# A spectral unit's frequency bins moved half a step: 93 groups for 102, contraction rows filled to 128, tables loaded beside x, matrix sums on two engines

## The chip, the cores and the metric

The kernel runs on one core of a Trainium2 chip. The metric is the device time in microseconds from launch to end. The kernel is one long program of eight stages in a row; the change touches the second of them only. TensorE (PE in the rows) multiplies, VectorE (DVE), ScalarE (ACT) and GpSimd (POOL) copy and compute, SyncE (SP) issues most of the transfers. The column PEclk gives the clock that TensorE was granted, 1.00 for 2.4 GHz and 0.50 for 1.2 GHz.

## The reference, cut to what matters

The second stage takes x as two-dimensional tokens (4 batches, 2304 tokens each, 128 channels), normalises every token, and runs a spectral unit over the token axis for four nested edges of the sequence. In essence:

```
Vf = rfft(phi, n);  Uf = rfft(u, n)           # phi: 2304 x 16 filters, u: b x 2304 x 128
U_plus  = irfft(Vf * Uf)                       # for every filter k and channel d
U_minus = the same for u * (+1, -1, +1, ...)
out  = einsum('btkd,k,kde->bte', U_plus,  sigma**0.25, M_phi_plus)
out += einsum('btkd,k,kde->bte', U_minus, sigma**0.25, M_phi_minus)
out += sum over i < 3 of shift(u, i) @ M_u[i]
```

There are four sets of matrices (M_phi, M_u); a running, weighted sum of them (weights from a softmax with gumbel noise) is what each of the four parts of the spectrum uses. The result is added to x.

## The kernel before, in words

`spectral_unit` (L1056) never forms a filtered signal per k. It evaluates both u and the taps at a set of frequencies ("bins"), builds for each bin a 128 x 128 matrix from taps and M, multiplies, and goes back. Time is written as 64 rows by 36 residues (ROWS_T, RES). Bins are grouped in slots of 36; SEG_SLOTS = (49, 25, 13, 9) slots serve four lengths, and each count is rounded up to a multiple of 3 (TRIO), so there are 17 + 9 + 5 + 3 = 34 trios, 102 slots.

The stage is a sequence of blocks with a barrier after each:

1. `branch_weights` (L1088): eight tiny loads, softmax weights.
2. `load_all`: the four parts of x, nothing else runs.
3. `norm_and_turn` (L138): layer norm on DVE, ACT and POOL. SP loads the tables meanwhile (phi, fa, sign, fe, the first matrices, far).
4. `to_bins` (L1130), the first half: PE turns the taps (L1202), ACT and DVE spread them (L1260, L1262, L1289), PE makes the taps' bins (L1210, contraction over 100 rows: real part in rows 0 to 35, imaginary part in rows 64 to 99), ACT scales and rounds each trio in two instructions (L1267, L1271), DVE takes the rest (L1293), SP stores it (L1340).
5. `to_bins`, the second half, in four phases (2 pairs of batches x 2 halves of the slots, 51 slots each). A phase first turns u (L1222, 16 groups of channels, 64 rows contracted, 51 columns) into tile ax, copied out by ACT (L1276) and DVE (L1298); then, once the last copy is done, bins it (L1234, 17 trios, 100 rows contracted, 72 columns), copied out by ACT (L1280) and DVE (L1302) and stored by SP (L1347).
   Beside it POOL makes the running matrix sum and its rounded high and low parts (L1310 to L1320). After each phase's stores SP stores the matrices to DRAM, the high part twice (six transfers, L1330 and L1331), and loads the next raw ones (L1333, L1334).
6. `mix_bins` (L1362): per trio and half of the output channels, PE fills tile mix (L1432: the matrix load has 105 rows, 216 columns) and multiplies by the bins (L1449), interleaved; ACT and DVE copy out. Both engines' copies are awaited in order by counters. At the first trio and at the three changes of segment ACT loads the matrices, half by half, one transfer of 105 rows by 32 KB for each half (L1503). PE waits for the half that it needs. Each trio's products go to DRAM and come back transposed, and are inverted two trios later (L1459).
7. `from_bins` (L1607): loads the result (L1637, one transfer of 96 rows and one of 6 for each piece), PE contracts it (L1667), DVE adds x (L1675), SP stores.

PE in these blocks follows an order written out by hand; each queue is in order.

Of the kernel before, what the change touches and what calls it, by code (L numbers as in the profile page):

```python
# [137 lines left out]
def norm_and_turn(nc, name, X, XN, eps, ident=None, out_of=None, stores=(), loads=()):  # L138
# [4 lines left out]
    with ExitStack() as ctx:  # L143
# [5 lines left out]
        ps = ctx.enter_context(nc.psum_tensor(name + "_ps", [P, 8, 512], F32))  # L149
        s = Signals(nc, name, "own var_ready std_ready shift_ready by_dve by_act by_pool turned held stored fetched")  # L150
# [14 lines left out]
        with nc.Block() as block:  # L165
            @block.sync
            def _(sp):
                for dst, src in loads:
                    sp.dma_start(dst, src).then_inc(s["fetched"], 16)
# [8 lines left out]
                if loads:  # L178
                    sp.wait_ge(s["fetched"], 16 * len(loads))
# [876 lines left out]
def spectral_unit(nc, x_dram, out_dram, w, scratch):  # L1056

    bins_dram, taps_dram = scratch("fq_bins", [TRIOS, P, 2, WORDS]), scratch("fq_taps", [TRIOS, TALL_M, COLS])
    mats_dram = scratch("fq_mats", [NEDGE, TALL_M, C * P])
    prod_dram, back_dram = scratch("fq_prod", [SLOTS_F * RES, 8, C]), scratch("fq_back", [RES, 2 * SLOTS_F, B * C])  # L1060
    with ExitStack() as ctx:
        def sb(name, shape, dt=F32):
            return ctx.enter_context(nc.sbuf_tensor("fq_" + name, shape, dt))

        wgt, root = sb("wgt", [P, NEDGE]), sb("root", [STACK, 1])
        branch_weights(nc, w, wgt, root)
        with ExitStack() as held:
            def part(name, shape, dt=F32):
                return held.enter_context(nc.sbuf_tensor("fq_" + name, shape, dt))

            U, turned = part("u", [P, G, 2, C]), part("ax", [P, HALF_SLOTS * 2 * C])
            fe, fa, sign = part("fe", [TALL, SLOTS_F, 2 * RES]), part("fa", [P, 2, SLOTS_F]), part("sign", [TALL, 1])
            far, far_r = part("far", [LAGS * TRIOS, LAGS * COLS]), part("far_r", [LAGS * TRIOS, LAGS * COLS], F32R)
            mats = [part("mats_" + n, [P, C * P // 4], dt) for n, dt in (("raw", F32), ("sum", F32), ("high", F32R), ("low", F32R))]
            lags = [part("lags_" + n, [32 * LAGS, C * P // 32], dt) for n, dt in (("raw", F32), ("sum", F32), ("high", F32R), ("low", F32R))]
            phi = turned[0:ROWS_T, SLOTS_F * STACK:SLOTS_F * STACK + RES * NK]
            flat = U[:, :, :, :].rearrange("p g t c -> p (g t) c")
            load_all(nc, "fq_load", [(flat[ROWS_T * (b % 2):ROWS_T * (b % 2) + ROWS_T, RES * (b // 2):RES * (b // 2) + RES, :],
                                      x_dram[b * S:(b + 1) * S, :].rearrange("(a r) c -> a r c", r=RES)) for b in range(B)])
            norm_and_turn(nc, "fq_ln", U[:, :, :, :], U[:, :, :, :], 1e-5, loads=[  # L1080
                (phi, w["phi"]), (fa[:, :, :], w["fa"]), (sign[:, :], w["sign"]), (fe[:, :, :], w["fe"]),
                (mats[0][:, :], w["mats"][0]), (lags[0][:, :], w["lags"][0]), (far[:, :], w["far"])])
            to_bins(nc, w, U, turned, fe, fa, sign, phi, far, far_r, mats, lags, wgt, root, bins_dram, taps_dram, mats_dram)
        mix_bins(nc, w, bins_dram, taps_dram, mats_dram, prod_dram, back_dram)
# [2264 lines left out]
```

## Time and profile before

| | us |
|---|---|
| median of 3 runs | 9376.89 (9366.43 to 9382.52) |
| the profiled execution | 9381.17 |
| its span, first to last instruction | 9378.6 |
| mean granted TensorE clock | 0.887 |

The profiled execution lies 4.3 us above the median of the runs; 2.6 us of it lie outside the span. The spectral unit takes from about 4225.9 to 6037.2 us of the span. A row of a table by stretches gives, after the length of the stretch, each engine's busy time with the number of its instructions in brackets, the granted clock, the mean busy share of the 16 DMA engines, and their GB/s.

### The profile page before, as it was taken

Reading aid. Unit: us, or ns where it says so; the run is one execution under the profiler, and the core shown is the slowest. Engines: PE = TensorE matmul, PEld = TensorE weight load, DVE = VectorE, ACT = ScalarE, POOL = GpSimd, SP = SyncE. Lnnn points to the kernel's source line nnn. Section 1 sums busy time; section 2 is a strip of 40 time slices with the busy share of each in tenths; the row PEclk is TensorE's granted clock in tenths of the full one; section 3 lists DMA queues with packets and bytes.
Section 4 is the critical chain, followed back from the end, with each engine's and each line's share of the span. In section 5 each row is a group of like instructions: output and inputs, shape, how many; then the busy total and the mean of one; then the engine's idle time right before and its main releaser. Section 6 shows DMA issues by size and latency. Waiting matters only on the chain. (4 is left out here: it accounts for less than half of the span.)

```text
span 9378.6 us, 167204 instructions
## 1 busy us (share of the span) xinstructions
PE 7377.9 (79%) x63268; PEld 4812.3 (51%) x63268; DVE 6500.1 (69%) x8252; ACT 4637.2 (49%) x8709; POOL 4163.0 (44%) x2920
## 2 busy tenths in 40 slices
PE   5877778777778777875799999388499989995667
PEld 3444444444444344444788888166355555553455
DVE  7999899998999799993166555232376656633447
ACT  4666566665666466652156555124224444452431
POOL 4999599995999499983300000000100000010001
PEclk8999999999999999995699999699679999997778
DMA  4555355553555355544332333621300010003000
GB/s 145 165 165 165 92 177 164 163 151 119 165 165 165 91 175 165 165 128 151 134 74 60 89 86 86 160 71 45 143 21 16 21 36 16 16 1 148 21 23 20
DMA packets 470862, 976.30 MB, mean 104 GB/s; under 512 B 127918, under 2 KB 226549, under 8 KB 452983
## 3 DMA queue, kind: packets, MB, share of 16 engines
q1 hardware_dynamic: 469098, 938.10, 33.6%
q10 hardware_dynamic: 960, 27.53, 1.1%
q8 instruction: 501, 8.21, 0.4%
q14 instruction: 303, 2.47, 0.1%
HBM read 822.05 MB, written 114.81 MB: 100 GB/s over the span
## 5 line engine op out<-in xcount | busy, mean ns | idle before, releaser
L892 POOL TENSOR_TENSOR ss_work<-ss_dtu,ss_ringb 128x768 f32<-128x768 f32 x1536 | 2759.6, 1822 | 260.0 <-POOLq L59 256.6
L754 PE MATMUL ss_ps<-ss_work,ss_ident 128*128 128x512 f32 (+1 forms) x6144 | 2307.9, 521 | 615.5 <-POOL ss_work L902 600.0
L754 PEld LDWEIGHTS ss_ps<-ss_work,ss_ident 128*128 128x128 f32 x6144 | 1201.0, 203 | 1503.5 <-issue 1319.0
L876 DVE TENSOR_TENSOR_SCAN ss_work<-ss_ps,ss_last,ss_work 128x768 f32<-128x768 f32 x1024 | 1808.6, 1800 | 64.2 <-ACT ss_ps L807 53.2
L807 ACT ACTIVATE ss_ps<-ss_dt,ss_a_neg 128x768 f32<-128x768 f32 x1536 | 1374.6, 895 | 288.1 <-DVE ss_work L876 270.9
L861 DVE TENSOR_TENSOR ss_work<-ss_work,ss_ps 128x1152 f32<-128x1152 f32 x768 | 1019.0, 1327 | 1.2 <-ACT ss_ps L815 1.2
L2655 DVE TENSOR_REDUCE at_top<-at_ps 128x1 f32<-128x384 f32 x1512 | 728.1, 546 | 402.5 <-PE at_ps L2573 402.3
L2636 ACT ACTIVATE at_probs<-at_ps 128x768 f32<-128x768 f32 x864 | 653.6, 808 | 660.4 <-PE at_ps L2592 659.4
L876 DVE TENSOR_TENSOR_SCAN ss_work<-ss_ps,ss_work 128x768 f32<-128x768 f32 x512 | 878.1, 1742 | 51.4 <-issue 18.0
L1409 DVE COPY mb_mix<-mb_ps 128x432 f32<-128x432 f32 x1088 | 634.4, 632 | 400.5 <-PE mb_ps L1432 400.4
L1499 ACT ACTIVATE mb_mix<-mb_ps 128x432 f32<-128x432 f32 x1088 | 612.6, 619 | 435.0 <-PE mb_ps L1432 429.0
L902 POOL TENSOR_TENSOR ss_work<-ss_work,ss_ringc 128x384 f32<-128x384 f32 x768 | 772.4, 1006 | 22.1 <-DVE ss_work L876 22.1
L1432 PE MATMUL mb_ps<-mb_taps,mb_mats 105*128 105x216 f32 x4352 | 668.1, 298 | 28.8 <-DMA mb_mats<-fq_mats 24.8
L2602 PE MATMUL at_ps<-at_probs,at_v 128*64 128x384 f32 x3456 | 663.5, 506 | 0.0
L1432 PEld LDWEIGHTS mb_ps<-mb_taps,mb_mats 105*128 105x128 f32 x4352 | 549.0, 196 | 128.3 <-issue 78.1
L2558 POOL COPY at_inv<-at_kept 32x384 f32<-32x384 f32 x80 | 39.9, 499 | 1224.3 <-ACT at_kept L2641 1222.7
L1449 PE MATMUL mb_ps<-mb_mix,mb_bins 128*8 128x64 f32 x29376 | 522.3, 221 | 30.7 <-issue 30.5
L1492 POOL COPY mb_bins<-mb_bins_by 128x432 f32<-128x432 f32 x34 | 20.3, 596 | 1182.6 <-PE mb_ps L1449 1049.6
L2573 PE MATMUL at_ps<-at_packs 96*128 96x384 f32 x1512 | 496.9, 379 | 19.6 <-DMA at_packs<-at_high 19.1
L813 ACT ACTIVATE ss_ps<-ss_ringc 128x512 f32<-128x512 f32 x768 | 462.7, 603 | 83.3 <-DVE ss_work L861 80.1
L2592 PE MATMUL at_ps<-at_packs 128*128 128x384 f32 x1728 | 453.0, 355 | 53.2 <-PEq L59 40.2
L1449 PEld LDWEIGHTS mb_ps<-mb_mix,mb_bins 128*8 128x8 f32 x29376 | 420.2, 90 | 94.8 <-issue 36.1
(554 smaller groups left out, 9917.5 us busy)
## 6 DMA issues: line engine op xcount, KB each, us to landing
ss_ringb<-scan_rows SPq DMA_DIRECT2D x768, 384.0 KB, 3.6
ss_ringc<-scan_rows SPq DMA_DIRECT2D x768, 384.0 KB, 3.9
c_w<-in_l_ffn_w SPq DMA_DIRECT2D x52, 1024.0 KB, 12.3
mb_mats<-fq_mats ACTq DMA_DIRECT2D x8, 3360.0 KB, 17.3
at_packs<-at_high SPq DMA_DIRECT2D x64, 288.0 KB, 5.5
fq_mats<-fq_mats_high SPq DMA_DIRECT2D x8, 2048.0 KB, 9.8
fq_bins<-tb_out SPq DMA_DIRECT2D x68, 216.0 KB, 1.9
mb_bins_by<-fq_bins SPq DMA_DIRECT2D x34, 432.0 KB, 3.9
```

The costliest lines, as they stand in the source:

```text
L754: return pe.matmul(acc[:, d * WIN + a:d * WIN + e], ident[:, :], weighed[:, t % DEEP, d, a:e], start=n == 0 and e - a == 512, stop=n == NS ...
L807: act.activation(decay[d], dt[:, i % 2, d, :], ACT.Exp, scale=a_neg[:, SECTIONS[i][0], d, n:n + 1]).then_inc(s["decayed"], 1)
L861: dve.tensor_tensor(weighed[:, t % DEEP, :, 0:SPLIT], hid[:, t % DEEP, :, 0:SPLIT], bc(spread_c[:, None, :], [P, D2, SPLIT]), ALU.mult).th ...
L876: dve.tensor_tensor_scan(hid[:, t % DEEP, d, ::step], decay[d][:, ::step], drive[:, t % DEEP, d, ::step], start, ALU.mult, ALU.add).then_i ...
L892: pool.tensor_tensor(drive[:, t % DEEP, d, :], dtu[:, t // NST % 2, d, :], ringb[:, t % RING, :], ALU.mult).then_inc(s["driven"], 1)
L902: pool.tensor_tensor(weighed[:, t % DEEP, :, SPLIT:WIN], hid[:, t % DEEP, :, SPLIT:WIN], bc(ringc[:, t % RING, None, SPLIT:WIN], [P, D2, W ...
L1409: copy(*fill_part(h, n)).then_inc(sem, 1)
L1432: ins = pe.matmul(ps[:, n % 4, e * COLS:(e + 1) * COLS], mats[:, first:first + P], taps[:, c % 2, :], start=True, stop=True, skip_group_ch ...
L1449: ins = pe.matmul(ps[32 * g:32 * g + 8, 4 + y % 2, at:at + HALF_E], bins[:, c % 2, n, 1 - m:3 - m, :].rearrange("p m b -> p (m b)"), mix[: ...
L2602: ins = pe.matmul(acc[64 * h:64 * h + 64, 0:R], v[:, j, 2 * pair + h, :, :].rearrange("p a d -> p (a d)"), probs[:, n % 4, h, :], start=j ...
L2636: act.activation(probs[:, n % 4, :, :], ps[:, 2 * (n % 2):2 * (n % 2) + 2, 0:R], ACT.Exp).then_inc(s["weighed"], 1)
L2655: dve.tensor_reduce(top[:, bass.ds(tile + h * NT_, 1), u], ps_bank(ps, 5 + g % 3)[:, 0:R], AX.X, ALU.max).then_inc(s["reduced"], 1)
```

## The change

- Bins at odd half steps. `frequency_tables` puts the frequencies at (2 f + 1) / 2 instead of f, so that no slot holds a bin that is its own mirror. SEG_SLOTS = (48, 24, 12, 9): 16 + 8 + 4 + 3 = 31 trios, 93 slots, with no slot left empty. The two halves of the slots are now 16 trios (48 slots) and 15 (45 slots).
- Contraction rows filled. Tables fe and sign get 128 rows (rows 36 to 63 and 100 to 127 of fe are zero); the turned tiles are copied out with 128 rows, and DVE blanks PSUM rows 32 to 63 and 96 to 127 first. L1234's and L1210's matmuls contract over 128 rows.
- Another order of blocks. `branch_weights`, the load of x and the taps' half of `to_bins` become one block, `taps_to_bins`, ahead of the layer norm. Everything that SP loads is issued at its start on SP's queue. Each tap trio is rounded by one ACT instruction and one DVE instruction that reads PSUM. The first matrices' sum is made at its end by DVE and ACT.
- Matrix sums on DVE and ACT, in five pieces, in the midst of the binning of phases 0 to 2; POOL does nothing there. The high part is stored once (four transfers), the raw load goes ahead of the stores.
- `mix_bins` reads the high part twice: six transfers where there was one. At the start the first half comes in four pieces, the first issued by ACT, the others, the bins and the second half by SP.
- `from_bins` splits the slots at 48: one transfer of 96 or 90 rows for each piece.

```diff
-SEG_SLOTS = (49, 25, 13, 9)
+SEG_SLOTS = (48, 24, 12, 9)
-SEG_TRIOS = tuple(-(-n // TRIO) for n in SEG_SLOTS)
+SEG_TRIOS = tuple(n // TRIO for n in SEG_SLOTS)
+PART_TRIOS = ((TRIOS + 1) // 2, TRIOS // 2)
+ROWS_K = P
-            fe, fa, sign = part("fe", [TALL, SLOTS_F, 2 * RES]), part("fa", [P, 2, SLOTS_F]), part("sign", [TALL, 1])
+        fe, fa, sign = part("fe", [ROWS_K, SLOTS_F, 2 * RES]), part("fa", [P, 2, SLOTS_F]), part("sign", [ROWS_K, 1])
+        taps_to_bins(nc, w, x_dram, ps, U, turned, fe, fa, sign, far, far_r, mats, lags, wgt, root, taps_dram)
+        norm_and_turn(nc, "fq_ln", U[:, :, :, :], U[:, :, :, :], 1e-5)
+        to_bins(nc, w, ps, U, turned, fe, fa, mats, lags, wgt, bins_dram, mats_dram)
...
+            def _(sp):                                   # taps_to_bins
+                for dst, src in ((phi, w["phi"]), (fa[:, :, :], w["fa"])):
+                    sp.dma_start(dst, src).then_inc(s["phi_loaded"], 16)
+                for dst, src in few:
+                    sp.dma_start(dst, src).then_inc(s["few_loaded"], 16)
+                sp.dma_start(sign[:, :], w["sign"]).then_inc(s["few_loaded"], 16)
+                sp.dma_start(fe[:, :, :], w["fe"]).then_inc(s["fe_loaded"], 16)
+                for b in range(B):
...
+                sp.dma_start(far[:, :], w["far"]).then_inc(s["far_loaded"], 16)
+                for dst, src in ((mats[0][:, :], w["mats"][0]), (lags[0][:, :], w["lags"][0])):
+                    sp.dma_start(dst, src).then_inc(s["mats_loaded"], 16)
+                for n in range(TRIOS):
+                    sp.wait_ge(s["lowered"], n + 1)
+                    sp.dma_start(taps_dram[n, 0:STACK, :], split[:, n % RING_T, :].bitcast(F32)).then_inc(s[stored[n % RING_T]], 16)
...
+                for n in range(TRIOS):                    # its ACT part
+                    act.wait_ge(s["made"], GROUPS_K + n + 1)
+                    if n >= RING_T:
+                        act.wait_ge(s[stored[n % RING_T]], 16 * (n // RING_T))
+                    act.activation(split[:, n % RING_T, :], bank(GROUPS_K + n)[0:STACK, 0:COLS], ACT.Copy, scale=root[:, :]).then_inc(s["rounded"], 1)
...
+                for rows in (slice(32, 64), slice(96, 128)):   # its DVE part
+                    dve.memset(ps[rows, :, :], 0.0).then_inc(s["blank"], 1)
...
+                    dve.scalar_tensor_tensor(low, bank(GROUPS_K + n)[TAPS:2 * TAPS, 0:COLS], root[TAPS:2 * TAPS, :], low, ALU.mult, ALU.subtract).then_inc(s["lowered"], 1)
+                dve.wait_ge(s["mats_loaded"], 32)
+                for q in range(PIECES):
+                    raw, total_m = pieces[q][0], pieces[q][1]
+                    dve.tensor_scalar(total_m, raw, wgt[0:raw.shape[0], 0:1], None, ALU.mult).then_inc(s["summed"], 1)
+                for q in range(PIECES):
+                    dve.wait_ge(s["cut"], q + 1)
+                    dve.tensor_tensor(pieces[q][3], pieces[q][1], pieces[q][2], ALU.subtract).then_inc(s["cut_low"], 1)
...
                         act.activation(*binned_part(ph, i), ACT.Copy).then_inc(s["by_act"], 1)
+                        if ph + 1 < NEDGE and i // 2 < PIECES:
+                            cut(ph, i // 2)
...
                         dve.tensor_copy(*binned_part(ph, i)).then_inc(s["by_dve"], 1)
+                        q = i // 2
+                        if ph + 1 < NEDGE and q < PIECES:
+                            if q + 1 < PIECES:
+                                gather(ph, q + 1)
+                            lower(ph, q)
-            @block.gpsimd
...
-                    for i, (source, source_l) in enumerate(((high, high_l), (high, high_l), (low, low_l))):
+                    for i in range(2):
+                        sp.dma_start(mats_dram[n, i, 0:TAPS, :].rearrange("j (q x) -> (j q) x", q=4), mats[2 + i][:, :].bitcast(F32)).then_inc(s["mats_stored"], 16)
+                        sp.dma_start(mats_dram[n, i, TAPS:TAPS + LAGS, :].rearrange("l (g x) -> (l g) x", g=32), lags[2 + i][:, :].bitcast(F32)).then_inc(s["mats_stored"], 16)
...
+        def load_mats(eng, n, first, end, sem):          # mix_bins
+            part = slice(first * PIECE, end * PIECE)
+            taps_high, taps_low = (mats_dram[n, i, 0:TAPS, part] for i in range(2))
+            lags_high, lags_low = (mats_dram[n, i, TAPS:TAPS + LAGS, part] for i in range(2))
+            at = 0
+            for source in (taps_high, taps_high, taps_low, lags_high, lags_high, lags_low):
+                rows = source.shape[0]
+                eng.dma_start(mats[at:at + rows, part].bitcast(F32), source).then_inc(sem, 16)
+                at += rows
...
-                load_mats(0, 0)
-                load_mats(0, 1)
+                load_mats(act, 0, 0, 1, s["mats_first"])
...
                 load_taps(0)
+                for q in range(1, FIRST_LOADS):
+                    load_mats(sp, 0, q, q + 1, first_loads[q])
                 load_bins(0)
+                load_mats(sp, 0, FIRST_LOADS, 2 * FIRST_LOADS, s["mats_second_half"])
...
-                            for lo, hi in ((0, 96), (96, SLOTS_F)):
-                                rows = back_dram[first:first + STEP, SLOTS_F * half + lo:SLOTS_F * half + hi, :].rearrange("i p x -> p i x")
-                                sp.dma_start(Z[lo:hi, n % RING_Z, half, u, :, :], rows).then_inc(s[loaded[n % RING_Z]], 16)
+                            rows = back_dram[first:first + STEP, PART_ROWS[0] * half:PART_ROWS[0] * half + PART_ROWS[half], :].rearrange("i p x -> p i x")
+                            sp.dma_start(Z[0:PART_ROWS[half], n % RING_Z, half, u, :, :], rows).then_inc(s[loaded[n % RING_Z]], 16)
```

## Rows read from the trace of the kernel before

**Rows 1.** By stretches: us; PE, PEld, DVE, ACT, POOL busy; PEclk, DMA share, GB/s.
```profile
4225.90:4235.20 9.30, 0.00 (x0) 0.00 (x0) 1.92 (x12) 2.08 (x5) 0.00 (x0) 0.50 0.02 1
4235.20:4261.10 25.90, 0.00 (x0) 0.00 (x0) 0.00 (x0) 0.00 (x0) 0.00 (x0) 0.50 0.86 182
4261.10:4295.40 34.30, 0.00 (x0) 0.00 (x0) 27.95 (x136) 8.24 (x22) 14.77 (x19) 0.50 0.64 168
4295.40:4346.80 51.40, 39.07 (x269) 38.18 (x270) 29.60 (x36) 30.35 (x71) 28.13 (x6) 0.50 0.20 56
4346.80:4388.10 41.30, 24.01 (x1025) 22.59 (x1025) 9.90 (x18) 8.78 (x18) 12.05 (x2) 0.58 0.61 231
4388.10:4431.50 43.40, 43.39 (x204) 43.40 (x204) 4.86 (x8) 4.24 (x8) 24.61 (x7) 0.50 0.22 83
4431.50:4470.80 39.30, 23.93 (x1026) 22.59 (x1025) 9.32 (x16) 8.72 (x17) 10.61 (x1) 0.68 0.63 242
4470.80:4512.20 41.40, 41.32 (x204) 41.28 (x204) 4.86 (x8) 4.24 (x8) 26.00 (x8) 0.53 0.24 86
4512.20:4552.90 40.70, 23.63 (x1025) 22.47 (x1024) 9.32 (x16) 8.71 (x17) 11.42 (x2) 0.81 0.61 234
4552.90:4594.50 41.60, 41.54 (x205) 41.44 (x205) 4.86 (x8) 4.24 (x8) 25.18 (x7) 0.53 0.23 86
4594.50:4632.20 37.70, 23.59 (x1027) 22.61 (x1027) 9.32 (x16) 8.73 (x17) 0.00 (x0) 0.75 0.49 192
4632.20:4674.80 42.60, 41.82 (x204) 41.62 (x203) 4.86 (x8) 4.77 (x9) 0.00 (x0) 0.52 0.23 84
...
4730.00:5907.00 1177.00, 1139.85 (x33419) 965.33 (x33418) 712.42 (x1226) 698.22 (x1258) 77.92 (x96) 0.99 0.30 76
5924.80:6037.20 112.40, 30.30 (x144) 5.94 (x144) 12.37 (x18) 0.00 (x0) 0.00 (x0) 0.56 1.00 218
```

**Rows 2.** SP in order of time, at two successive trios of the mixing.
```profile
5003.17 0.33 SPq L1547 DMA_DIRECT2D mb_taps<-fq_taps  x1
...
5036.87 0.33 SPq L1547 DMA_DIRECT2D mb_taps<-fq_taps  x1
```

**Rows 3.** PE in order of time, within the turning of u: start, length, idle before.
```profile
4358.36 2.97 PE L1222 MATMUL tb_ps<-fq_fa,fq_u 64*36 64x51 f32 x127 [4.70 <-issue]
...
4544.77 2.89 PE L1222 MATMUL tb_ps<-fq_fa,fq_u 64*36 64x51 f32 x127 [0.60 <-issue]
```

**Rows 4.** Transfers from 4346 to 4380 us: KB each, us from issue to landing.
```profile
fq_taps<-fq_ax SPq DMA_DIRECT2D x3, 81.0 KB, 2.5
fq_lags_raw<-in_l_ffn_lags SPq DMA_DIRECT2D x1, 192.0 KB, 18.9
```

**Rows 5.** Three lines alone by stretches, the binning (L1234), L2140 and L2299.
```profile
4552.90:4555.30 2.40, 2.34 (x21) 2.37 (x22) 1.00 0.03 7
...
6547.30:6563.90 16.60, 16.24 (x144) 16.11 (x144) 1.00 0.02 8
...
6649.00:6677.00 28.00, 28.00 (x143) 28.00 (x143) 0.50 0.01 2
```

**Rows 6.** Instructions of L2140 and L2299: count, ns, rows by columns.
```profile
L2140 PE MATMUL c1p_ps<-c1p_wt,c_xn x144: 222/275/323, 6547.3 to 6563.8; 128*128 128x64 f32 x144
...
L2299 PE MATMUL c1s_ps<-c1s_rows,c_weights x144: 417/417/578, 6648.6 to 6677.2; 64*128 64x128 f32 x144
```

**Rows 7.** The matmuls of the taps' bins: ns min, median, max; first and last.
```profile
L1210 PE MATMUL tb_ps<-fq_fe,fq_ax x204: 367/368/435, 4313.0 to 4346.5; 100*96 100x72 f32 x102
```

**Rows 8.** From the page, a long DVE tensor operation: busy, mean ns, idle before.
```profile
L861 DVE TENSOR_TENSOR ss_work<-ss_work,ss_ps 128x1152 f32<-128x1152 f32 x768 | 1019.0, 1327 | 1.2 <-ACT ss_ps L815 1.2
```

**Rows 9.** PE in order of time, at the start of mixing and a change of segment.
```profile
4712.76 2.05 PE L1432 MATMUL mb_ps<-mb_taps,mb_mats 105*128 105x216 f32 x8 [1.79 <-DMA mb_mats<-fq_mats]
...
5268.55 0.63 PE L1432 MATMUL mb_ps<-mb_taps,mb_mats 105*128 105x216 f32 x2 [4.00 <-issue]
```

**Rows 10.** From the page, the matrices' loads: count, KB each, us to landing.
```profile
mb_mats<-fq_mats ACTq DMA_DIRECT2D x8, 3360.0 KB, 17.3
```

More of the change, by code:

```diff
@@ L1058, in spectral_unit @@
     bins_dram, taps_dram = scratch("fq_bins", [TRIOS, P, 2, WORDS]), scratch("fq_taps", [TRIOS, TALL_M, COLS])
-    mats_dram = scratch("fq_mats", [NEDGE, TALL_M, C * P])
+    mats_dram = scratch("fq_mats", [NEDGE, 2, TAPS + LAGS, C * P])
     prod_dram, back_dram = scratch("fq_prod", [SLOTS_F * RES, 8, C]), scratch("fq_back", [RES, 2 * SLOTS_F, B * C])
[L1061 to L1071, printed above, removed]
-            fe, fa, sign = part("fe", [TALL, SLOTS_F, 2 * RES]), part("fa", [P, 2, SLOTS_F]), part("sign", [TALL, 1])
[L1073 to L1084, printed above, removed]
@@ new lines, in spectral_unit, with matrix_pieces, taps_to_bins @@
+    mix_bins(nc, w, bins_dram, taps_dram, mats_dram, prod_dram, back_dram)
+    from_bins(nc, w, back_dram, x_dram, out_dram)
+def matrix_pieces(mats, lags):
+    width = C * P // 16
+    return [[m[:, q * width:(q + 1) * width] for m in mats] for q in range(4)] + [[m[:, :] for m in lags]]
+PIECES = 5
+def taps_to_bins(nc, w, x_dram, ps, U, turned, fe, fa, sign, far, far_r, mats, lags, wgt, root, taps_dram):
+    GROUPS_K, RING_T = NK // 4, 8
+    flat = U[:, :, :, :].rearrange("p g t c -> p (g t) c")
+    taps = turned[:, 0:SLOTS_F * STACK].rearrange("p (n k) -> p n k", k=STACK)
+    phi = turned[0:ROWS_T, SLOTS_F * STACK:SLOTS_F * STACK + RES * NK]
+    by_lag = phi.rearrange("a (r k) -> a r k", k=NK)
+    at = SLOTS_F * STACK + RES * NK
+    split = turned[0:STACK, at:at + RING_T * COLS].rearrange("p (n x) -> p n x", x=COLS).bitcast(F32R)
+    pieces = matrix_pieces(mats, lags)
+    sigma = w["sigma"].rearrange("(k a) -> k a", a=1)
@@ L1099, in branch_weights @@
-        s = Signals(nc, "bw", "own max_ready exp_ready root")
-        with nc.Block() as block:
+        lw, gum, e = sb("lw", [P, NEDGE]), sb("gum", [P, NEDGE]), sb("e", [P, NEDGE])
+        mx, total, hard, count = sb("mx", [P, 1]), sb("total", [P, 1]), sb("hard", [P, NEDGE]), sb("count", [P, NEDGE])
+        ones = sb("ones", [P, NEDGE])
+        stored = [f"stored{n}" for n in range(RING_T)]
+        s = Signals(nc, "tt", " ".join(["own few_loaded phi_loaded fe_loaded x_loaded far_loaded mats_loaded blank max_ready exp_ready root made by_act by_dve copied spread rounded lowered far_rounded far_stored weighted summed cut cut_low", *stored]))
@@ new lines, in _ @@
+                dve.wait_ge(s["copied"], 1)
+                dve.tensor_copy(taps[:, :, TAPS:2 * TAPS], taps[:, :, 0:TAPS]).then_inc(s["spread"], 1)
+                for n in range(TRIOS):
+                    dve.wait_ge(s["rounded"], n + 1)
+                    low = split[TAPS:2 * TAPS, n % RING_T, :]
+                    dve.scalar_tensor_tensor(low, bank(GROUPS_K + n)[TAPS:2 * TAPS, 0:COLS], root[TAPS:2 * TAPS, :], low, ALU.mult, ALU.subtract).then_inc(s["lowered"], 1)
+                dve.wait_ge(s["mats_loaded"], 32)
@@ new lines, in to_bins @@
+def to_bins(nc, w, ps, U, turned, fe, fa, mats, lags, wgt, bins_dram, mats_dram):
+    CG = C // 8
+    RING_B = 4
+    PHASES = 4
+    flat = U[:, :, :, :].rearrange("p g t c -> p (g t) c")
+    ax = turned[:, :].rearrange("p (n r c) -> p n r c", r=2, c=C)
+    pieces = matrix_pieces(mats, lags)
+    starts = [0]
+    for ph in range(PHASES):
+        starts.append(starts[-1] + 2 * CG + PART_TRIOS[ph % 2])
+    def owner(n):
+        ph = max(p for p in range(PHASES) if starts[p] <= n)
+        v = n - starts[ph]
@@ L1184, in ax_free @@
         def ax_free(eng, ph):
-            eng.wait_ge(s["made"], turned_at(ph, 0, 0))
-            if ph == 0:
-                for n in range(RING_T):
-                    eng.wait_ge(s[stored_t[n]], 16 * len(range(n, TRIOS, RING_T)))
+            if ph:
+                eng.wait_ge(s["made"], turned_at(ph, 0, 0))
         with nc.Block() as block:
```

333 lines of the change are left out of this document (161 added, 172 removed).

## The prediction, made before the changed kernel was run

> **What bounds the kernel now.** I read the granted clock and the page first, then cut the spectral unit into stretches by its barriers, then looked at PE in order of time in each, and last at the transfers. All that the change touches lies between 4225.9 and 6037.2 us. The table by stretches [rows 1] shows four different limits, and the reader should see them apart.
> - Up to 4346.8 us there is a serial chain: tiny loads 9.3, x 25.9 with no engine at work, layer norm 34.3, taps 51.4. Sum 120.9 us.
> - Then four phases, each a turning of u (41.3, 39.3, 40.7 and 37.7 us, PE busy in 24 of them) and a binning (43.4, 41.4, 41.6, 42.6 us, PE busy throughout, yet at clock 0.50 to 0.53). The turning is held by PE's instructions not coming: "issue" gaps of 4.7 us while the DMA engines carry the matrices, 0.6 us when they don't [rows 3].
> - The mixing, 1177 us, is PE at clock 0.99, 97% busy, 33.7 us for a trio (5036.87 - 5003.17 [rows 2]).
> - The last block, 112.4 us, has a DMA share of 1.00: bytes bound it.
>
> **Fewer trios in the mixing.** 34 become 31 with nothing else changed within a trio: 3 x 33.7 = -101 us. Nothing hides it, since PE is the bound.
>
> **Its matrix loads.** The bytes stay; one transfer of 105 rows becomes six, issued by ACT between copies that PE waits for. At a change of segment a half takes 17.3 us to land [rows 10], about PE's half trio of 33.7 / 2, and the gap that PE shows there is one for its instructions, 4.00 us [rows 9], not one for the matrices. Five more issues at about 0.33 us (the issue time of rows 2) hold ACT 1.7 us, six times; most is covered by four banks of PSUM. I take +3 us (0 to +25 if landing grows by 4 us in each of the six). At the start, the second half decides: PE got past it at 4712.76 [rows 9], 38 us after the binning's end, for 6.9 MB plus bins. The first half in pieces lets PE begin earlier and then wait for the same landing. So the early start is worth nothing; I take +3 us (-3 to +9) for smaller transfers.
> A rule of the Trainium skill speaks against this part (page "DMA: Bandwidth & Descriptors", section "Why a DMA increments its semaphore by 16 and not by 1"): a copy is spread over the largest number of engines, at most 16, that divides its outer sizes. By it the 3-row parts sit on three engines, which then carry 9 rows in place of 7 for each half; as an estimate from that page and rows 10, landing goes from 17.3 to 22 us. By that the start would lose 8 us and the changes of segment next to nothing. No row of before has such a 3-row load.
>
> **Fewer and other binnings.** A phase had 17 trios of 12 matmul records; 204 in 43.4 us [rows 1] is 213 ns each at clock 0.50, 2.56 us for a trio. With 62 for 68: 6 x 2.56 = -15 us. DVE and ACT get the matrix sums here: pieces of 1024 columns cost 1.2 us on DVE (1.33 us for 1152 [rows 8]); ACT has one such piece where DVE has two. Beside one 0.61 us copy (4.86 us for 8 [rows 1]) for two trios, DVE has 3.0 us of work in 5.1 us. Hidden, at the low clock.
>
> **The clock in the binning.** This is the disputed step. In the high stretch 22 records took 2.40 us, 109 ns each [rows 5], half the price. Phases 1 to 3 began high, but by their means of 0.53, 0.53 and 0.52 over 41 to 43 us [rows 1] they were high for 2 to 3 us only. Which streams of short matmuls keep the clock? L2140 has 128 rows and 64 columns and kept 1.00 for all of its 16.6 us; L2299 has 64 rows and 128 columns, more column time, and stayed at 0.50 for 28 us, fully busy [rows 5, 6]. The binning has 100 rows and 72 columns. So rows seem to count, and with 128 it is closer to the stream that kept its clock. But neither row shows such a stream climbing by itself from 0.50; it has to enter high, over the short wait for the last copies. Turnings were at 0.58, 0.68, 0.81 and 0.75 on average [rows 1], so perhaps half of the phases enter high and hold. A phase that holds saves 15.5 trios x 1.28 = 20 us, less the 2 us that it had: 18 us. I take two: -36 us (0 to -72). In such a phase DVE's 3.0 us stand against PE's 2.6 for two trios, for five pairs: 2 us late, taken up by eight banks.
> The Trainium skill's rule (page "TensorE: Matmul & The Clock Gate", section "Part 1: The HAM clock gate") is that sustained activity releases the throttle, without a word on rows. The trace disagrees: PE is busy for 43.39 of 43.40 us at 0.50. By the rule as written the filled rows would change nothing, and the step would be worth 0 instead of -36.
>
> **The turning.** 48 or 45 columns for 51 change nothing, since PE waits for instructions. The transfers beside it go from 9.2 MB (three stores of 2.1 MB with three thin ones of 0.2, and a raw load of 2.3) to 6.9, in the last phase from 6.9 to 4.6. At the free pace (2.9 + 0.6 us for two groups [rows 3], 8 times) a turning takes 28 us; the four took 159, 47 us more, for 34.4 MB. In proportion to bytes 25.3 MB cost 34: -13 us (-25 to 0). ax has 128 rows for 100 in its copies: columns set the copy time, no cost.
>
> **The head.** Now one block. SP puts 10.9 MB on its queue at once (fe 3.4, x 4.7, matrices 2.3, rest), at 182 to 212 GB/s: 55 us. The taps took 17.6 us from the block's start to their first binning (4295.4 to 4313.0 [rows 1, 7]); a second blanking of 4096 columns adds at most 4.7 us by L861's rate [rows 8], so eight trios are binned by 30 us. Then the ring of eight is full, and its stores stand in SP's queue behind the loads, as fq_lags_raw's 192 KB took 18.9 us behind the matrices where 81 KB took 2.5 on a queue nearly idle [rows 4]. At 57 us the stores land. PE is ahead by eight banks; 15 trios are left at 6 x 164 ns (204 in 33.5 us [rows 7]), 15 us: 72. DVE reaches the matrices only then: five sums and five differences, 10 us: 82; stores of far and the barrier: 86. Then the layer norm, 34.3, as before: 120. Against 120.9: 0 us (-12 to +12). What was to hide behind the load of x is late again for the queue's order. No loads run beside the norm, which gains nothing: DVE and POOL bound it.
>
> **The last block.** It is bound by bytes: 15.0 MB of 24.5 shrink by 9/102, 1.3 MB at 218 GB/s [rows 1] is -6 us, and the 6-row transfers go: -7 us (-12 to -3).
>
> **Sum**, against the profiled execution: -101 + 3 + 3 - 15 - 36 - 13 + 0 - 7 = -166 us. From 9381.2 that is 9215; the median of the runs is 4.3 us lower: 9211 us.
>
> **Rivals.**
> 1. The clock stays low in all binnings, because one drop lasts to the phase's end: -130 us, 9247. For it: each of the three high entries fell within 3 us [rows 1]; the skill's rule above gives the same. Against: L2140.
> 2. The clock holds in all four: -202 us, 9175. For it: less traffic makes the turnings denser, so they enter high more often. Against: the first turning was mostly low.
> 3. The matrix loads land late and PE waits, +4 us in six halves and +9 at the start instead of +6 together, with the head 12 us longer and at most one phase high: 9275. For it: six transfers for one, all to be landed. Against: the gap at a change names PE's instructions, not the matrices [rows 9].
> 4. Slower than before: the clock falls at a change of segment and doesn't come back in the mixing. At half the clock a trio takes at most 67.4 us, 33.7 more. From five such trios on the whole gain is gone; if it were ten of the fifteen after the first change, 337 us: 9548. For it: longer waits for instructions at a change (4.00 us [rows 9]) are what the clock would fall after. Against: the mean clock of the mixing is 0.99 [rows 1], so it came back each time.
> 5. That the change does not do what it says, fewer trios at another period: each trio does the same work, so I give it nothing of its own.
>
> **Chances.** Forecast (one to three phases high) 0.42; none 0.28; all four 0.16; rival 3 0.12; rival 4 0.02. The forecast's own range is 9188 to 9237. The range that should hold the time 8 times in 10 takes in rivals 1 and 2: 9168 to 9265. About 0.2%, 19 us, is what can be told from no change. Faster 0.97, within 0.2% 0.01, slower 0.02.
>
> **What would show it.** In the mixing 31 taps loads at 33.7 us: wrong if the period moves. In the binnings PEclk and the length: about 20 us at 1.00, 40 at 0.50; the first microseconds of each tell whether it entered high. In the turnings fewer gaps over 3 us. In the head: the first tap stores landing after the matrices; if they land early, the block ends 10 to 15 us sooner. At the start of the mixing PE's wait before the second half, at about 34 us after the first issue. The forecast fails if the layer norm starts later than 95 us after the block's start, or if PE waits for mb_mats at the changes.

## The result and the profile after

The changed kernel takes 9313.35 us (median of 14 runs, 9266.97 to 9338.35) where the kernel before takes 9379.95 (14 runs, 9345.20 to 9400.23): ratio 0.9927, 95% interval 0.9913 to 0.9940. That is 67 us faster, not the 169 us of the forecast (9211), and outside its range of 9168 to 9265. The profiled execution took 9326.6 us, its span is 9324.8.

The changed kernel by stretches, answering [rows 1] (columns as there). In order: the head's block, the layer norm, four times turning and binning, the wait for the matrices, the first trio, the rest of the mixing, the last block.

```profile
4228.70:4309.80 81.10, 31.32 (x250) 30.73 (x250) 32.57 (x58) 24.73 (x46) 0.00 (x0) 0.58 0.63 170
4309.80:4342.40 32.60, 0.00 (x0) 0.00 (x0) 27.96 (x136) 8.19 (x21) 14.75 (x18) 0.50 0.00 1
4342.40:4381.30 38.90, 23.68 (x1024) 22.40 (x1024) 8.96 (x17) 7.84 (x16) 0.00 (x0) 0.50 0.49 180
4381.30:4422.50 41.20, 41.14 (x193) 41.04 (x193) 14.78 (x17) 8.53 (x13) 0.00 (x0) 0.50 0.22 82
4422.50:4459.60 37.10, 23.49 (x1025) 22.38 (x1024) 9.20 (x18) 7.53 (x16) 0.00 (x0) 0.71 0.51 195
4459.60:4497.20 37.60, 37.56 (x182) 37.46 (x182) 14.75 (x17) 8.00 (x12) 0.00 (x0) 0.52 0.23 83
4497.20:4535.00 37.80, 23.55 (x1025) 22.31 (x1025) 9.01 (x17) 8.39 (x17) 0.00 (x0) 0.64 0.51 191
4535.00:4576.10 41.10, 41.09 (x192) 41.01 (x192) 14.72 (x17) 8.53 (x13) 0.00 (x0) 0.50 0.22 82
4576.10:4612.30 36.20, 23.68 (x1025) 22.44 (x1024) 9.13 (x17) 7.53 (x16) 0.00 (x0) 0.59 0.35 136
4612.30:4651.00 38.70, 38.65 (x180) 38.47 (x180) 4.25 (x7) 3.71 (x7) 0.00 (x0) 0.50 0.22 81
4651.00:4668.90 17.90, 0.00 (x0) 0.03 (x1) 0.91 (x1) 0.53 (x1) 0.00 (x0) 0.50 0.77 169
4668.90:4722.80 53.90, 32.19 (x561) 29.71 (x561) 19.77 (x33) 18.92 (x34) 4.84 (x6) 0.62 0.48 100
4722.80:5833.10 1110.30, 1036.71 (x29890) 879.34 (x29886) 644.31 (x1108) 628.31 (x1137) 70.58 (x87) 0.96 0.31 74
5867.90:5974.40 106.50, 31.16 (x144) 5.95 (x144) 12.38 (x18) 0.00 (x0) 0.00 (x0) 0.56 1.00 218
```

Three things are to be seen. No binning was at a clock above 0.50 for more than 2 us. The first trio takes 53.9 us, with PE busy in 32 of them. The mixing's clock is 0.96 where it was 0.99, and PE is busy for 1037 of 1110 us (93%, before 97%).

The mixing again, before and after, from the second trio to the last fill: PE's groups with their idle time and what ended it. First the kernel before.

```profile
L1432 PE MATMUL mb_ps<-mb_taps,mb_mats 105*128 105x216 f32 x4220 | 642.7, 296 | 4.0 <-issue 4.0
L1449 PE MATMUL mb_ps<-mb_mix,mb_bins 128*8 128x64 f32 x28488 | 506.4, 221 | 26.2 <-issue 26.0
L1459 PE MATMUL mb_ps<-mb_prod_t,mb_fi 72*100 72x512 f32 x192 | 107.7, 643 | 0.1
```

The changed kernel:

```profile
L1491 PE MATMUL mb_ps<-mb_taps,mb_mats 105*128 105x216 f32 x3839 | 592.7, 298 | 32.4 <-ACT mb_mix L1562 17.3 <-issue 14.4 <-DVE mb_mix L1468 0.7
L1508 PE MATMUL mb_ps<-mb_mix,mb_bins 128*8 128x64 f32 x25920 | 463.7, 222 | 22.0 <-issue 22.0
L1518 PE MATMUL mb_ps<-mb_prod_t,mb_fi 72*100 72x512 f32 x174 | 98.5, 648 | 19.1 <-DMA mb_fi<-in_l_ffn_fi 19.1
```

Idle time goes from 30 to 74 us, and nobody names the matrices. Four single rows of PE and ACT in the changed kernel tell where: at the mixing's start, then at the second and third change of segment.

```profile
4704.90 2.04 PE L1491 MATMUL mb_ps<-mb_taps,mb_mats 105*128 105x216 f32 x8 [20.43 <-DMA mb_mats<-fq_mats]
...
5562.83 0.54 ACT L1562 ACTIVATE mb_prod<-mb_ps 104x448 f32<-104x448 f32 x1 [18.98 <-DMA fq_prod<-mb_prod]
...
5564.34 1.62 PE L1491 MATMUL mb_ps<-mb_taps,mb_mats 105*128 105x216 f32 x6 [12.98 <-ACT mb_mix L1562]
...
5733.19 2.03 PE L1518 MATMUL mb_ps<-mb_prod_t,mb_fi 72*100 72x512 f32 x2 [19.15 <-DMA mb_fi<-in_l_ffn_fi]
```

ACT waits 19 us to reuse a product buffer, because a 14 KB store has not landed; PE waits for ACT; PE waits for an 84 KB load. These small transfers share the DMA engines with the six loads of a half. (With one load for a half it can happen too, more seldom: in the run f3 below PE waited 13.2 us for the same 84 KB load.)

Away from the changes the period is what it was [rows 2]: SP's loads of taps in the changed kernel, two undisturbed ones and then across the first change (45.7 and 48.4 us).

```profile
4992.59 0.33 SPq L1608 DMA_DIRECT2D mb_taps<-fq_taps  x1
5026.26 0.33 SPq L1608 DMA_DIRECT2D mb_taps<-fq_taps  x1
...
5195.92 0.33 SPq L1608 DMA_DIRECT2D mb_taps<-fq_taps  x1
5241.60 0.33 SPq L1608 DMA_DIRECT2D mb_taps<-fq_taps  x1
5290.00 0.33 SPq L1608 DMA_DIRECT2D mb_taps<-fq_taps  x1
```

Below, "excess" is the sum over all trios but the last of (start of the next trio's first fill - start of its own - 33.7 us). It is 48 us before and 120 after, 20 of them in the first trio. It is read from the one profiled execution of each kernel. Kernels that load their matrices alike differ by up to 11 us (changed, e3 and e4: 120, 111, 113; e2, f2, f4 and g4: 55, 47, 58, 47; before and f3: 48, 58).

### The profile page after: what moved, and what is told of

Its sections match the earlier page's. It is cut to its first block and busy times, and to the rows that moved or that the text cites. A ratio compares the mean times of both kernels' runs of the same rounds, so it can differ in the third digit from the quotient of the medians.

```text
span 9324.8 us, 160533 instructions
## 1 busy us (share of the span) xinstructions
PE 7266.0 (78%) x60184; PEld 4717.3 (51%) x60184; DVE 6468.1 (69%) x8177; ACT 4579.4 (49%) x8574; POOL 4017.7 (43%) x2881
## 5 line engine op out<-in xcount | busy, mean ns | idle before, releaser
L872 DVE TENSOR_TENSOR_SCAN ss_work<-ss_ps,ss_work 128x768 f32<-128x768 f32 x512 | 878.9, 1745 | 51.7 <-issue 17.3
L1468 DVE COPY mb_mix<-mb_ps 128x432 f32<-128x432 f32 x992 | 578.8, 631 | 427.0 <-PE mb_ps L1491 426.7
L1562 ACT ACTIVATE mb_mix<-mb_ps 128x432 f32<-128x432 f32 x992 | 557.2, 617 | 442.5 <-PE mb_ps L1491 437.1
L1491 PE MATMUL mb_ps<-mb_taps,mb_mats 105*128 105x216 f32 x3968 | 617.6, 300 | 72.0 <-DMA mb_mats<-fq_mats 39.6
L1491 PEld LDWEIGHTS mb_ps<-mb_taps,mb_mats 105*128 105x128 f32 x3968 | 507.8, 198 | 164.9 <-issue 81.8
L1508 PE MATMUL mb_ps<-mb_mix,mb_bins 128*8 128x64 f32 x26784 | 478.7, 222 | 25.3 <-issue 25.3
L2655 PE MATMUL at_ps<-at_packs 128*128 128x384 f32 x1728 | 452.2, 354 | 53.8 <-PEq L59 40.0
L1508 PEld LDWEIGHTS mb_ps<-mb_mix,mb_bins 128*8 128x8 f32 x26784 | 386.0, 91 | 83.3 <-issue 30.8
```

Of the source, the lines that this page charges most:

```text
L872: dve.tensor_tensor_scan(hid[:, t % DEEP, d, ::step], decay[d][:, ::step], drive[:, t % DEEP, d, ::step], start, ALU.mult, ALU.add).then_i ...
L1468: copy(*fill_part(h, n)).then_inc(sem, 1)
L1491: ins = pe.matmul(ps[:, n % 4, e * COLS:(e + 1) * COLS], mats[:, first:first + P], taps[:, c % 2, :], start=True, stop=True, skip_group_ch ...
L1508: ins = pe.matmul(ps[32 * g:32 * g + 8, 4 + y % 2, at:at + HALF_E], bins[:, c % 2, n, 1 - m:3 - m, :].rearrange("p m b -> p (m b)"), mix[: ...
```

## The experiments

Ratios are to the kernel before, with their 95% intervals; landing is from the first to the last packet of the first half of the matrices at the first change of segment, in the profiled execution.

| kernel | runs | median us | ratio | excess | landing us |
|---|---|---|---|---|---|
| changed | 14 | 9313 | 0.9927 (0.9913-0.9940) | 120 | 24.7 |
| e1, 32+16+16+16+16+9 rows | 12 | 9323 | 0.9954 (0.9937-0.9971) | 160 | 28.0 |
| e2, one of 105 rows | 6 | 9225 | 0.9860 (0.9835-0.9884) | 55 | 14.2 |
| e3, x on ACT's queue | 6 | 9303 | 0.9930 (0.9906-0.9954) | 111 | 24.0 |
| e4, 16 long matmuls | 3 | 9299 | 0.9928 (0.9900-0.9956) | 113 | 23.5 |
| e5, before + six loads | 6 | 9436 | 1.0065 (1.0049-1.0082) | 100 | 24.4 |
| f2, six of 105 rows, by columns | 5 | 9217 | 0.9834 (0.9816-0.9852) | 47 | 14.8 |
| f3, before + 16 long | 8 | 9368 | 0.9993 (0.9978-1.0007) | 58 | 15.2 |
| f4, e2 + 4 long | 5 | 9186 | 0.9805 (0.9785-0.9824) | 58 | 14.2 |
| g1, 32+32+32+9 rows | 4 | 9255 | 0.9879 (0.9861-0.9898) | 100 | 20.4 |
| p1, 0-63, 64-95, 96-104 | 2 | 9271 | 0.9899 (0.9875-0.9922) | 113 | 19.8 |
| p2, 0-31, 32-95, 96-104 | 2 | 9254 | 0.9881 (0.9856-0.9905) | 63 | 15.7 |
| g4, f4 + matmuls at the start | 5 | 9192 | 0.9813 (0.9797-0.9829) | 47 | 14.1 |

The kernel before has an excess of 48 and a landing of 15.6 us.

**e1: no three-row loads.** Edit:

```
-            for source in (taps_high, taps_high, taps_low, lags_high, lags_high, lags_low):
+            for source in (taps_high, taps_high[0:half], taps_high[half:TAPS], taps_low[0:half], taps_low[half:TAPS], mats_dram[1][n, :, part]):
```

> The changed kernel, still with six loads for each half of the matrices, but no part of 3 rows: 32, 16, 16, 16, 16 and one of 9 (the lags' high sums are stored twice for it, 0.2 MB more a segment). Theory A, three-row parts: in the changed kernel a half took 24 us to land (5214.0 to 5238.0) instead of 17.3, with three 3-row copies one after another at the end while the DMA share fell; PE's instructions and the product stores stood behind them, and the clock fell. By A a half lands in 17 us, the sum of the trios' excess over 33.7 us goes from 120 back to about 50, the kernel 50 to 70 us faster than the changed one: ratio to before 0.987. Rival B, the number of transfers (ACT issues for 2.8 us instead of 0.3, six landings to wait for): no change, 0.993. Rival C, chance of the clock at each change: within 10 us of the changed kernel, with other trios long.

Measured: not faster than the changed kernel but, if anything, slower (the two intervals just touch), excess 160. My first theory fell: without a 3-row part a half lands still later, after 28.0 us. The stretches of the trace say why; first the 32-row part of e1, then its 16-row parts.

```profile
5182.40:5187.20 4.80, 4.10 (x117) 3.54 (x114) 2.41 (x4) 2.28 (x5) 0.55 (x1) 1.00 1.06 220
5187.20:5205.00 17.80, 7.03 (x134) 6.14 (x135) 3.20 (x6) 2.20 (x4) 0.00 (x0) 0.62 1.06 130
```

The DMA engines are full in both, but 16-row parts move 130 GB/s where the 32-row part moves 220.

**e2: one load of 105 rows.** Edit, with the stores as in the kernel before:

```
-            for source in (taps_high, taps_high, ...): eng.dma_start(mats[at:at + rows, part]..., source)
+            eng.dma_start(mats[:, part].bitcast(F32), mats_dram[n, :, part]).then_inc(sem, 16)
```

> The changed kernel with the matrices stored as before (high sums twice, six stores, 35 rows more a segment) and loaded by one transfer of 105 rows for a half (one for each quarter of the first half). A and B both expect the excess of the trios back at about 50 us and 50 to 70 us gained, less 3 us for the stores in the turnings: ratio to before 0.987. C expects no change. If it is faster than the run with six loads of 16 or 32 rows, the difference is the number of transfers.

Measured: 0.9860, excess 55. The loads' form so costs some 65 us of excess. That the median fell by 88 us and not by 65 has two more reasons in the trace: PE's first fill came 9.7 us after the last binning (17.9 in the changed kernel), and three binnings held the high clock, of which more under e4. The same stretch of time in the changed kernel (32-row parts, then the 3-row ones) and in e2:

```profile
5214.10:5229.20 15.10, 7.91 (x189) 6.88 (x190) 4.44 (x8) 3.60 (x7) 0.42 (x1) 0.76 0.98 205
...
5229.00:5238.00 9.00, 8.68 (x238) 7.54 (x237) 4.84 (x9) 4.92 (x9) 0.00 (x0) 0.82 0.66 111
```

```profile
5162.60:5176.00 13.40, 11.32 (x264) 8.65 (x264) 6.23 (x11) 5.51 (x10) 0.00 (x0) 0.90 0.99 262
```

205 and then 111 GB/s against 262. With its stores as before (six transfers for four) the turnings took 158.4 us again, where the changed kernel has 150.0. The other traces divide in the same way: kernels with the six stores (f2, f4, g4, p1, p2) have 158 to 160 us, those that store the high part's 32 rows once (e1, e3, e4, g1) 147 to 150.

**e5 and f2: the number of loads against the rows they span.** e5 takes the kernel before and cuts its load in six by rows; f2 takes e2 and cuts it in six by columns:

```
+                    for lo, hi in ((0, TAPS), (TAPS, 2 * TAPS), (2 * TAPS, STACK), (STACK, STACK + LAGS), ...):   # e5
+                        act.dma_start(mats[lo:hi, part].bitcast(F32), mats_dram[n, lo:hi, part])...
+                for q in range(6):                                                                                # f2
+                    part = slice(first * PIECE + 1408 * q, min(first * PIECE + 1408 * (q + 1), end * PIECE))
```

> The kernel before, each half of the matrices loaded by six transfers (32, 32, 32, 3, 3 and 3 rows) in place of one of 105; nothing else. Theory D (the rate of a transfer goes by how many rows of SBUF it spans: with 105 rows 262 GB/s in the changed kernel with one load, with 32 rows 203 to 220, with 16 rows 130): the trios' excess over 33.7 us goes from 48 to 100 or more at the changes and 15 us come at the start, so the kernel before gets 50 to 70 us slower, ratio 1.006. Theory B (the number of transfers): the same here. Rival E (it is the source in DRAM, where the changed kernel reads the same rows twice and from another stride): no change here, since the source stays as it was, ratio 1.000.

> The changed kernel with the matrices stored as before and each later half loaded by six transfers of all 105 rows, each of 1408 of the 8192 columns. By D as fast as with one load of 105 rows: excess about 55 us, ratio 0.986 (0.984 to 0.989). By B (six issues by ACT, six landings) as slow as the changed kernel: excess 100 to 120 us, ratio 0.992 or more.

Measured: e5 is 61 us slower than the kernel before (1.0065): 52 us more excess, and PE's first fill 33.0 us after the last binning where it was 23.0. So this one edit, alone, costs what the changed kernel lost. The source in DRAM was untouched, so it is not the source. f2 issues six loads as well and is as fast as e2 (0.9834), so it is not the number of transfers either. Left are the rows that a load spans in SBUF, the memory that the kernel's tiles lie in.

**p1 and p2: which rows.** `cuts = (0, 64, 96, 105)` against `(0, 32, 96, 105)` in e2.

> Each later half loaded as rows 0 to 63, 64 to 95 and 96 to 104, from the array as stored before. The Trainium skill (page SBUF, section on the DMA port swizzle) says that partitions 0 to 63 reach the same 8 ports as 0 to 31, and 32 to 95 all 16. By it the 64-row load moves at the 32-row load's rate, 205 GB/s, 10 us. Rival (the rate goes by the number of rows alone): 64 rows at some 235 GB/s, 9 us, and the same in the next kernel.

> The same three sizes in another place: rows 0 to 31, 32 to 95 and 96 to 104. By the port map the 64-row load now moves at the rate of the 105-row one, 262 GB/s, in 8 us, 2 us less than where it spans rows 0 to 63; a half lands 2 us earlier and the kernel is 0 to 15 us faster. By the number of rows alone: no difference between the two.

Within the 64-row load, p1 and p2:

```profile
5176.20:5180.80 4.60, 0.82 (x17) 0.53 (x16) 1.00 (x2) 1.09 (x2) 0.00 (x0) 0.81 1.01 207
```

```profile
5209.80:5214.20 4.40, 0.94 (x18) 0.65 (x17) 1.12 (x2) 1.09 (x2) 0.00 (x0) 0.77 1.10 432
```

The same 64 rows' worth of bytes: 207 GB/s into rows 0 to 63, 432 into rows 32 to 95, where the expectation had 262. Excess 113 against 63. So the number of rows alone doesn't set the rate. The times (9271 and 9254, two runs each) can't be told apart: in p1's profiled run two binnings held the high clock, in p2's none, which makes up for most of the difference in excess. The Trainium skill's map (page "SBUF — State Buffer", section "Door 1: The DMA port swizzle (why `[64,N]` ≈ `[32,N]`)") gives rows 0 to 15 four ports of sixteen, 0 to 31 and 0 to 63 eight, 64 to 127 the other eight; the trace agrees with 130 GB/s for 16-row loads, 205 for 32 rows and 207 for rows 0 to 63, and with 432 where rows 32 to 95 take in both eights. The map alone doesn't explain one load of 105 rows, which takes in both eights as well and ran at 262; why is not shown.

**g1: the 3-row tail apart.** One load of 9 rows for three of 3.

> The changed kernel with the three 3-row loads of a half made one of 9 rows (the lags' high sums stored twice for it), so four loads: 32, 32, 32 and 9. It parts the cost of the 32-row spans from that of the 3-row tail. If the spans cost most, three of them take 3 x 5.1 us at 205 GB/s and the 9 rows 3 us, landing about 19 us in place of 24 (and 13.4 with one load): excess of the trios 85 to 95 us, ratio 0.990. If the three 3-row loads were all of the cost: excess 55, ratio 0.986. If they cost nothing: excess 115 to 120, 0.993.

Measured: excess 100, landing 20.4. Of the 65 us between 120 and 55 the 3-row loads make 20 (11 by the 111 of e3, which has the same loads as the changed kernel), the 32-row spans some 45.

The table's last two columns read together: a half has half a trio, 33.7 / 2 = 16.9 us, to land before PE comes to it. The kernels that land in 14.1 to 15.7 us have an excess of 47 to 63, those that take 19.8 to 28.0 have 100 to 160.

**e3: x on another queue.** The loads of x, far and the first matrices issued by ACT (`sp.dma_start` becomes `act.dma_start`).

> The changed kernel with the loads of x, of the far taps and of the first matrices issued by ACT, so that the tap stores on SP's queue stand only behind fe. Theory A (a queue's order): the ring of eight is not held up, PE's gap of 18.8 us in the taps' binning goes, the layer norm begins 15 to 20 us earlier (65 us after the block's start instead of 81), time 15 to 20 us less than the changed kernel. Rival (the 16 engines are full, the stores wait for bytes whatever their queue): the norm begins at 78 to 81 us, no change in time.

Measured: no gain that can be told (0.9930). PE's gap in the taps' binning did go, but its work begins later; the changed kernel, then e3:

```profile
4280.40 12.40 PE L1154 MATMUL fq_ps<-fq_fe,fq_ax 128*96 128x72 f32 x90 [18.76 <-DVE fq_ax L1213]
```

```profile
4248.81 5.18 PE L1138 MATMUL fq_ps<-fq_fa,fq_ax 64*36 64x93 f32 x64 [24.08 <-DMA fq_fa<-in_l_ffn_fa]
4276.00 20.18 PE L1148 MATMUL fq_ps<-fq_fe,fq_ax 128*96 128x72 f32 x186 [22.00 <-DMA fq_fe<-in_l_ffn_fe]
```

On two queues the loads that PE needs first, fa and fe, share the engines with x. The layer norm begins 81.5 us after SP's first load (4313.2 - 4231.7), as in the changed kernel (4309.8 - 4228.8 = 81.0): the rival's number held. What the gap gave back went into the waits for these two. An order that spares both was not run.

**e4 and f3: the clock at the binning's door.** In both, ahead of each binning (f3 in the kernel before, with 100 rows):

```
+                    for _ in range(16):
+                        pe.matmul(bank(binned_at(ph, 7))[:, 0:512], ax[:, 0, 0, :], fe[:, :, :].rearrange("p n x -> p (n x)")[:, 0:512], ...)
```

> The changed kernel with 16 matmuls of 512 columns, whose result is not used, before the first trio of each binning. They cost 16 x 0.43 to 0.85 us in each of four phases, 27 to 54 us. Theory of the prediction (a stream of 128 rows keeps the clock if it enters high): binnings of 22 to 25 us in the phases that enter high, the kernel 0 to 45 us faster than the changed one. Rival (this stream of short matmuls falls whatever it enters with): high for a few us only, binnings of 36 to 40 us, the kernel 20 to 50 us slower.

> The kernel before, whose binning has 100 rows, with 16 matmuls of 512 columns, whose result is not used, ahead of each binning, as in the run with 128 rows, where all four binnings then ran at clock 1.00 in 20.2 to 21.5 us. If the rows filled are what keeps the clock (the prediction's choice): high for 2 to 4 us and then 0.50, binnings of 39 to 42 us, the kernel 45 to 60 us slower than before. Rival (rows don't matter, only the state at entry): binnings of 22 to 23 us at 1.00, the kernel 20 to 30 us faster than before.

One binning of e4 (128 rows), then in f3 the long matmuls and the binning after them (100 rows):

```profile
4468.89:4489.04 20.15, 20.15 (x182) 20.07 (x180) 13.27 (x16) 8.35 (x12) 0.00 (x0) 1.00 0.39 144
```

```profile
4387.57:4401.38 13.81, 13.81 (x32) 6.16 (x33) 0.00 (x0) 0.00 (x0) 13.66 (x5) 1.00 0.00 1
4401.38:4424.21 22.83, 22.83 (x206) 22.75 (x204) 4.86 (x8) 4.25 (x8) 12.25 (x4) 1.00 0.40 146
```

Every binning that was entered so ran at 1.00 to its end, 20.2 to 21.5 us with 128 rows and 22.8 with 100. So the rows are not what holds it. Without the long matmuls, of the 32 binnings in the eight profiled kernels that have 128 rows and none of them (changed, e1, e2, e3, f2, g1, p1, p2) 10 held, 0 to 3 in one kernel. Of the 8 with 100 rows (before, e5) one did:

```profile
4630.39:4653.40 23.01, 22.97 (x204) 22.82 (x204) 4.86 (x8) 4.25 (x9) 0.00 (x0) 1.00 0.40 146
```

Nor is it enough to begin high. Of the other 22 binnings with 128 rows 11 were at 1.00 for their first 0.3 to 1.6 us and then at 0.50 to the end, and so were three in the kernel before and three in e5, for 1.2 to 2.5 us. Two phases of e2: the one fell after 1.5 us, the next held.

```profile
4441.29:4442.79 1.50, 1.50 (x14) 1.50 (x14) 1.09 (x1) 0.00 (x0) 0.00 (x0) 1.00 0.04 11
4442.79:4478.56 35.77, 35.77 (x173) 35.64 (x174) 13.62 (x16) 8.00 (x12) 0.00 (x0) 0.50 0.24 87
...
4517.13:4538.76 21.63, 21.63 (x196) 21.56 (x199) 14.36 (x17) 8.88 (x13) 0.00 (x0) 1.00 0.40 145
```

With long matmuls right ahead of it, 16 or four, the stream held in 16 of 16 phases (e4, f3, f4, g4). Without them 10 of 21 that began high held with 128 rows and one of seven with 100; whether the rows shift the chance is not settled by so few.

Each that holds saves 17 to 20 us. The time itself fell little in e4 and not measurably in f3, since 16 long matmuls cost 13.8 us a phase and more. In f3's profiled run the binnings with their long matmuls took 20 us less than before, of which the mixing gave back 10 (excess 58 for 48).

**f4: both repairs**, e2 with four long matmuls for 16.

> The changed kernel with both repairs: one load of 105 rows for each half or quarter, and 4 matmuls of 512 columns ahead of each binning (0.86 us each at the high clock, twice that at the low one, 14 to 28 us in all). If four are enough to enter high, all binnings take 20.2 to 21.5 us: 0 to 20 us faster than one load alone, ratio 0.985, and less scatter between runs. If not, 15 to 25 us slower than one load alone, ratio 0.988.

The first phase of f4: the four long matmuls, then the binning.

```profile
4381.06:4386.26 5.20, 5.20 (x8) 2.19 (x9) 1.04 (x1) 0.00 (x0) 0.00 (x0) 0.67 0.00 0
4386.26:4407.75 21.49, 21.49 (x194) 21.41 (x192) 13.27 (x16) 8.88 (x13) 0.00 (x0) 1.00 0.40 146
```

Four are enough: they take 3.5 to 5.2 us a phase, and all four binnings ran at 1.00, as did the four of g4. 9186 us, ratio 0.9805, the lowest median here, and 188 us below the kernel before (9374.7 in that series).

**g4: matmuls while the matrices load.**

> The kernel with one load for each half or quarter and four long matmuls ahead of each binning, and now also 32 matmuls of 216 columns, whose result is not used, at the start of the mixing, where PE waits for the first matrices anyway. There the first trio took 45.4 us with the clock high for 0.28 of it, where 33.7 is the period. If the clock is up when the first matrices are there: first trio 34 to 38 us, 5 to 12 us faster, ratio 0.979. Rival (the wait for the second half sets the end of the first trio anyway): no change, 0.9805. If the 32 outlast the wait: 0 to 5 us slower.

Measured: 0.9813, not told apart from f4. The first trio took 39.4 us for 45.4, but it began later: PE passed the wait for the second half 37.8 us after the last binning in f4 (4635.8 - 4598.0) and 35.2 us in g4 (4640.8 - 4605.6). PE still waited 7.9 us for the second half there: its landing sets the end, as the rival had it.

## Why the prediction was wrong, point by point

In the profiled executions (span 9324.8 - 9378.6 = -53.8 us; the profiled run of the changed kernel is 13 us above its median):

| term | forecast | measured |
|---|---|---|
| three trios fewer | -101 | -101 |
| matrix loads at the changes | +3 | +53 |
| start of the mixing | +3 | +15 |
| binnings, fewer and clock | -15 - 36 | -10 |
| turnings | -13 | -9 |
| head | 0 | -7 |
| last block | -7 | -6 |
| outside the unit, gap before the last block | 0 | +11 |

The time fell 112 us less than forecast in these executions: 62 us of it are the matrix loads (50 at the changes of segment, 12 at the start), 41 the binnings, 4 the turnings, and the rest nearly cancels.

- **Its matrix loads: the step that failed.** "I take +3 us (0 to +25 ...)" for the changes; they cost 1110.3 - (1158.2 - 101.1) = +53. I saw that a half landed in about PE's half trio [rows 10], so that nothing was to spare, and then asked only whether PE would wait for the matrices. It didn't: ACT waited for product stores and PE for its instructions and a small load, behind the same engines. So the sign of failure that it named, PE waiting for mb_mats at the changes, never showed, though the step had failed. Rival 3 had the cause (loads landing late) and put it at +4 us a half with PE waiting for them; it is 9 us a half.
- The rule of the Trainium skill weighed there (page "DMA: Bandwidth & Descriptors", section "Why a DMA increments its semaphore by 16 and not by 1": 3-row parts on three engines; the estimate from it was a landing of 22 us for 17.3) was of use: by the packets the landing went from 15.6 to 24.7. The trace agrees with a tail at 111 GB/s, and g1 gives it 11 to 20 us of excess. But "the changes of segment next to nothing" was wrong by 50 us, and the larger part, 32 rows at 205 GB/s, I had not looked for.
- **The start**: +15 for +3. PE began 17.9 us after the last binning instead of 23.0, and then waited 20.4 us for the second half, which it passed 49.8 us after the first issue and not at about 34.
- **The clock in the binning: the second step that failed.** The price was right: a phase that holds is worth about 18 us (measured 17 to 20). The condition was wrong: "half of the phases enter high and hold" takes the one for the other, and 11 of 21 that began high fell. In the profiled run one began high, fell after 1.1 us and none held, which is rival 1; over the eight kernels 1.25 of 4 did, not two. That the filled rows are what keeps the clock is refuted by f3, where 100 rows kept it in four of four. Much of the scatter of the changed kernel, 9267 to 9338, has the size of three or four such phases; that the single runs differ by just that was not seen, as they have no trace, and f4, where all four hold, still scatters over 29 us.
- **Fewer binnings** gave 6 x 2.56 us, less about 5 us because two of the three phases that had begun high no longer did. The matrix sums on DVE and ACT cost nothing, even at the high clock: 20.15 us for 180 matmuls with them, 20.3 for 180 without (e2's last phase).
- **The turnings**: -9 for -13. e2, with the old stores, took 158.4 and not 150.0: the stores are the cause. That it is their bytes more than their number is likely, as e1 and g1, with a fifth small store, stayed at 150 and 149.
- **The head**: right in its steps. The norm began 81 us after the block's start (86 forecast); the gap of 18.8 us for the ring of eight is the one described. That the block ends 10 to 15 us sooner without that gap is not borne out by e3, where fe landed later instead.
- **The last block** is as forecast.

What stays open: what separates the binnings that began high and held from those that began high and fell, why one load of 105 rows stays at 262 GB/s where 64 well-placed rows reach 432, and why the stages outside the unit took 12 us more in the profiled run.

## What to carry to other kernels

Before one transfer is cut in several, ask which rows of SBUF each piece spans, not only how many bytes and issues there are: cut by columns, or so that a piece has rows on both sides of row 64. Where a load's landing just fits its cover, price its lengthening by all that shares the DMA engines (stores, small loads, instructions), since the wait shows up under their names. And where a long stream of short matmuls runs at the low clock, a few long matmuls right ahead of it can be cheap: here 3.5 to 6.5 us bought 17 to 20. Beginning high by itself is no assurance.

## What the runs showed of the hardware that was not expected

- A load from DRAM into rows 32 to 95 ran at 432 GB/s over 4.4 us, all traffic of the stretch counted; 105 rows in one load reached 262, rows 0 to 63 207, 32 rows 205 to 220, and the stretch of 16-row loads 130.
- The same stream of short matmuls (128 rows by 72 columns, PE busy without a gap) ran 41 us at clock 0.50 or 21.5 at 1.00, to the phase's end. After long matmuls it held 1.00 in 12 of 12 phases; of 21 that merely began at 1.00, 11 fell within 1.6 us.
- A 14 KB store held ACT for 19 us while six larger loads were in flight on another engine's queue.
